# Shifting 128 rows by one partition: one transfer of 127 rows, or one of 126 and one of 1

## The reference

```
def shift_token(t):
    t1, t2 = jnp.split(t, 2, axis=-1)
    t2 = jnp.pad(t2, ((0, 0), (1, 0), (0, 0)))[:, :-1]
    return jnp.concatenate([t1, t2], axis=-1)
...
x = x + o @ wo
h = shift_token(x)
mu = h.mean(-1, keepdims=True)
var = h.var(-1, keepdims=True)
h = (h - mu) / jnp.sqrt(var + 1e-05) * lg + lb
h = h @ w1 + b1
a, g = jnp.split(h, 2, axis=-1)
h = a * jax.nn.gelu(g, approximate=False)
x = x + h @ w2 + b2
```

## Time and profile before

| | |
|---|---|
| time, median of 3 runs | 2962.85 us (2961.32 to 2963.24) |
| time of the profiled execution | 2961.68 us |
| its span, first to last instruction | 2959.4 us |
| busy, share of the span | PE 96%, DVE 74%, ACT 56%, POOL 35% |
| chain that ended last | PE 75%, DVE 11%, DMA 6% (`e_hs<-x` 4%), POOL 3%, ACT 2% |
| transfers into `e_hs` | 64 of 127 rows (63.5 KB), 56 of one row (0.5 KB) |

### The profile page before, as it was taken

One profiled execution on the slowest core, in us unless ns is written; L12 is line 12 of the kernel. 1 busy time (PEld: TensorE's weight loads), 2 busy tenths in 40 slices (PEclk: granted clock), 3 DMA queues, 4 the chain that ended last, 5 costly groups with the idle time before them and its releaser, 6 DMA issues.

```text
span 2959.4 us, 52471 instructions
## 1 busy us (share of the span) xinstructions
PE 2835.6 (96%) x20384; PEld 1908.3 (64%) x20384; DVE 2176.4 (74%) x5057; ACT 1653.3 (56%) x3488; POOL 1048.7 (35%) x1208
## 2 busy tenths in 40 slices
PE   8998999999999999999997899999999899999997
PEld 7777877333333333333336788888878788888886
DVE  7885545788788778868846777777867577788784
ACT  3222332665565666556664576666666666666662
POOL 5333432033113212511314344434454444444441
PEclk9999999999999999999997999999999999999998
DMA  2000010321321322132203000000010100000001
GB/s 78 23 9 22 8 22 3 43 24 17 35 26 12 39 24 26 17 46 26 37 1 98 5 5 5 4 5 5 11 37 14 31 21 4 18 5 12 12 11 59
DMA packets 46284, 66.64 MB, mean 23 GB/s; under 512 B 9662, under 2 KB 34260, under 8 KB 46036
## 3 DMA queue, kind: packets, MB, share of 16 engines
q1 hardware_dynamic: 46036, 63.29, 12.0%
HBM read 24.99 MB, written 8.39 MB: 11 GB/s over the span
## 4 chain that ended last, share of the span: by engine, by line
PE 75%; DVE 11%; DMA 6%; POOL 3%; ACT 2%; issue 1%; SPq 1%; POOLq 0%; DVEq 0%; ACTq 0%
PE ps L1394 17%; PE pw L218 13%; PE ps L218 11%; PE pw L1381 10%; PE ps L1180 5%; DMA e_hs<-x 4%; PE pw L1180 4%; PE ps L1554 4%; PE pw L1467 2%; PE pw L1505 2%; PE pw L1330 1%; PE pw L1487 1%; DVE stat L1837 1%; DVE e_ot L2132 1%; PE ps L1467 1%
## 5 line engine op out<-in xcount | busy, mean ns | idle before, releaser
L1682 ACT ACTIVATE c_p<-pw 128x512 f32<-128x512 f32 x1024 | 562.3, 595 | 341.2 <-PE ps L1364 183.5
L1394 PE MATMUL ps<-c_p,c_vals 128*64 128x512 f32 x2048 | 547.4, 618 | 2.7 <-ACT c_p L1682 1.4
L1968 DVE TENSOR_REDUCE c_mx<-ps 128x1 f32<-128x512 f32 x694 | 462.7, 683 | 114.3 <-PE ps L1364 106.7
L1381 PE MATMUL pw<-c_qst,c_kst 50*128 50x512 f32 x1024 | 385.1, 449 | 9.4 <-DMA c_qst<-c_mr 9.0
L1381 PEld LDWEIGHTS pw<-c_qst,c_kst 50*128 50x128 f32 x1024 | 154.5, 185 | 368.2 <-ACT c_p L1682 272.1
L1364 PE MATMUL ps<-c_kst,c_qst 48*128 48x512 f32 x694 | 289.5, 452 | 4.6 <-DMA c_kst<-shared 3.5
L1736 ACT ACTIVATE e_sm<-e_sm,e_mx 128x256 f32<-128x256 f32 x512 | 253.9, 498 | 62.0 <-DVE e_mx L2113 61.9
L1968 DVE TENSOR_REDUCE c_mx<-pw 128x1 f32<-128x512 f32 x330 | 225.5, 683 | 47.3 <-PE pw L1364 43.8
L2233 POOL TENSOR_SCALAR stat<-stat 128x1 f32<-128x1 f32 (+1 forms) x138 | 32.1, 233 | 623.4 <-DVE stat L1840 352.0
L1394 PEld LDWEIGHTS ps<-c_p,c_vals 128*64 128x64 f32 x2048 | 104.2, 135 | 181.2 <-issue 162.1
L218 PE MATMUL pw<-shared,e_xb 128*128 128x512 f32 x792 | 216.9, 412 | 2.2 <-DVE e_xb L2062 1.5
(11 more groups left out here) (316 smaller groups left out, 6441.0 us busy)
## 6 DMA issues: line engine op xcount, KB each, us to landing
c_kst<-shared SPq DMA_DIRECT2D x192, 64.0 KB
c_qst<-shared SPq DMA_DIRECT2D x64, 128.0 KB
x<-in_L_attn_x SPq DMA_DIRECT2D x8, 512.0 KB, 3.8
c_qst<-shared SPq DMA_DIRECT2D x64, 64.0 KB
keep<-x SPq DMA_DIRECT2D x8, 512.0 KB, 4.5
e_raw<-keep SPq DMA_DIRECT2D x8, 512.0 KB, 3.5
out<-x SPq DMA_DIRECT2D x8, 512.0 KB, 5.9
e_hs<-x SPq DMA_DIRECT2D x64, 63.5 KB
```

Source lines behind the costliest of these rows:

```text
L1381: e.matmul(bank_of("c_s", n, sh, kt, h), c_kst[i][p0:p0 + 50, sh // 2, 128 * kt:128 * kt + 128], c_qst[i][p0:p0 + 50, sh // 2, 512 * h:512 ...
L1394: ins = e.matmul(pv[64 * h:64 * h + 64, :], c_v[:, kt, 33 * hd:33 * hd + 64], p[:, 512 * h:512 * h + 512], start=kt == 0, stop=kt == 7, sk ...
L1682: e.activation(c_p[slot["c_p", (n, sh, kt)]][:, 512 * h:512 * h + 512], bank_of("c_s", n, sh, kt, h), ACT.Exp, scale=0.5).then_inc(SC, 1)
L1968: e.tensor_reduce(c_mx[m % 2][:, qt, h:h + 1], bank_of("c_max", n, sh, qt, h), AX.X, ALU.max).then_inc(VE, 1)
```

## The change

The 127 rows go as two transfers, 126 and 1, and the row of the tile above is issued last instead of first. The count that the waits look for rises by 16. The planner's 2.6 us stays.

```
-                    P.land(f"hs{slot['d_hs', (l, win)]}", 2 if win % 8 else 1, "d_hs", l, win)
+                    P.land(f"hs{slot['d_hs', (l, win)]}", 3 if win % 8 else 2, "d_hs", l, win)
...
                 w.wait_ge(*dve("d_wo", l, win))
+                e.dma_start(hs[1:127, :], x[0:126, win, 128:256]).then_inc(landed, 16)
+                e.dma_start(hs[127:128, :], x[126:127, win, 128:256]).then_inc(landed, 16)
                 if win % 8:
                     e.dma_start(hs[0:1, :], x[127:128, win - 1, 128:256]).then_inc(landed, 16)
-                e.dma_start(hs[1:128, :], x[0:127, win, 128:256]).then_inc(landed, 16)
```

## The result

| | before | changed |
|---|---|---|
| median of the runs | 2963.05 us (2961.32 to 2963.34) | 2921.60 us (2920.62 to 2922.86) |
| ratio, 95% interval | | 0.9862 (0.9844 to 0.9879) |
| time of the profiled execution | 2961.68 us | 2921.17 us |
| its span | 2959.4 us | 2919.3 us |

41 us faster, where 32 were forecast. On another chip (chip 9 of the experiments) the changed kernel came to about the same time, 2922.82 us, but the one before ran at 2956.69; the ratio there is 0.9883 (0.9869 to 0.9896), 34 us.

The account below looks back on a forecast made before the run. PE bounds the kernel, so only PE's gaps behind DVE's waits for shifted rows, or loads queued behind them, count: 24.6 us of gaps plus 6.3 of clock make 30.9, giving 2931 us, range 2918 to 2947.

Parts of the forecast that it names:

- One shift: Stage d, from SP's first issue until the shifted rows are there: 3.2 us instead of 5.61, 2.4 us earlier.
- first load: PE's gap of 6.17 us at 1612.37, behind a weight load sharing an engine with the 127 rows: 2.85 us gained.
- 1674: PE's gap of 2.58 us at 1674.42, where `e_rp` stands behind the statistics: 2.4 us gained.
- 2194: PE's gap of 1.62 us at 2194.36, `e_qn` right behind the statistics: the whole gap, 1.6 us, gained.
- gaps handed on: Rival, chance 0.18: PE meets ACT, POOL or a load a little later instead; half the sum, 2946 us.
- 2302: PE's gap of 4.84 us at 2302.88, where DVE waited 6.66 us for the shift: 2.9 us gained.
- the five equal gaps: Second layer, PE's gap of 1.77 us at 2465.14 and four alike every 83 us: 1.55 each, 7.75 us.
- last shift: PE's gap of 4.32 us at 2909.10, where `e_hf` stands behind the last shift: 2.4 us gained.
- The clock: Matmuls run slower after some PE gaps; with those gaps gone or short, 6.3 us come back.
- more than the gaps: Rival, chance 0.08: gaps left out shorten too and the clock stays up at both ends; 10 us more, 2921.
- the slower case: Rival, chance 0.04: last row comes later than the 127 rows did, beyond 1.38 us per issue and pause; 2984 us.
- Hidden anyway: Rival, chance 0.04: every gap moves to another wait within its block of four windows; within 5.9 us of before.

Follow-up runs that it names:

- chip 9: Second chip for the changed kernel, unaltered, against the kernel before: 2922.82 us against 2956.69, ratio 0.9883.
- 64 and 63: Changed kernel with the 127 rows split as 64 and 63 instead of 126 and 1, row of the tile above last: 2921.75 us, ratio 0.9880 against before.
- chips 11 and 9: Kernel before, unaltered, run again on chip 11: 2957.87 us, ratio 1.0001; changed kernel, unaltered, run again on chip 9: 2922.82 us.
- the one at a lower clock: Against the kernel before, only the order changed, 127 rows issued before the row of the tile above: 2944.25 us, ratio 0.9962; its profiled execution took 2968.94 us.
- 113 and 14 rows: Against the kernel before, the 127 rows go as 113 and 14, row of the tile above last: 2942.29 us, ratio 0.9947.

## Why the prediction was right, and what was mis-sized

**One shift.** Forecast 3.2 us, measured 3.14. Two errors met: the big issue takes 0.81 us and not 0.60, the last row is there 1.70 us after its issue and not 2.0. The reading by divisors held for 126 and 113 rows in the traffic, and for 64 and 63 in the time. By the Trainium skill's rule ("DMA: Bandwidth & Descriptors", "Why a DMA increments its semaphore by 16 and not by 1"), 126 rows go over 14 engines and 113 over one; the share of up to eight tenths and the 2.9 us at 22 GB/s agree. The Trainium skill's advice on the same page ("Rules for kernel authors") against two transfers to disjoint partitions gives as its reason that both halves use all 16 engines. One transfer of 127 rows doesn't, so the advice doesn't carry over: not splitting costs 34 to 41 us here. The Trainium skill's fixed cost of about 2.0 us on that page, from which the prediction worked out a loss of some 5 us, stands there as a fit for transfers issued from GpSimd; end to end these costs don't come, since three overlapping transfers from SP took 3.14 us.

**The gaps.** Forecast 24.6 us, measured 24.8 of PE's idle time. That close a sum is partly luck, since the single terms miss in both directions:
- first load: 2.85 forecast, 6.17 - 4.25 = 1.9. SP's load now starts 1.62 us after the first issue instead of 0.76, 0.86 later and not 0.58, since the big issue grew; and it lands 4.09 us after its issue, not 3.44 as when alone:

```profile
1602.43 17.35 SPq L2406 DMA_DIRECT2D e_raw<-in_L_ffn_w  x7
...
1606.52 0.42 ACT L1593 ACTIVATE e_w<-e_raw 124x256 fp32r<-124x256 f32 x1 [3.51 <-DMA e_raw<-in_L_ffn_w]
```

- 1674: 2.4 forecast, 2.58. 2238 and 2356: 1.25 and 1.3, both gone.
- 2194: 1.6 forecast. The gap is gone, but 0.95 for `e_pt` is new just before, and the wait for `e_xb` behind it grew from 1.2 to 2.22. So nothing was won at this place. This is the "gaps handed on" of the rivals, at one place.
- 2302: 2.9 forecast, 1.9. DVE still waits 4.26 us for this shift, where 6.66 were.
- the five equal gaps: 1.55 each forecast, 1.55 each measured (1.77 to 0.2). In the stretch 2409 to 2900, with the small waits, 13.7 of idle time became 1.9: 11.8, where the terms had about 9.6. The small waits there are worth more than counted.
- last shift: 2.4 forecast. 4.32 became 1.89 as forecast, but the next gap for `e_hp` grew from 1.95 to 2.84: 1.5.

**The clock.** This is the term that was mis-sized: 6.3 us forecast. PE's busy time fell by 12.8 us (9.9 between the profiles of chips 11 and 9), and the granted clock says how much of it is clock. The two levels are 1.00 (2.4 GHz) and 0.50 (1.2 GHz). Cut into slices of 1 us, the busy time of each slice times (1 - its clock) is an estimate, from the traces, of what the lower level added to PE's work: 23.8 us before and 13.4 after, so 10.4 less. By stage it is 2.4, 0, 3.1, 3.4 and 1.4 us less. On chips 11 and 9 it is 20.2 and 13.5, 6.7 less.

Where it came from, on the first chip: what the prediction counted whole came back, 1.5 us at 1674 and 3.4 after two of the five gaps. The low clock after 2302.88 it counted half and it went whole, 3.0 us. After 1612 and at the end, where it counted nothing, 1.0 and 1.4 came back. After the gap of 1.88 us at 2287.96 the clock fell too (0.57 from 2288 to 2292), which the prediction hadn't seen; the gap is still there, but the clock no longer falls, 1.7 us. Against that, the grown gap for `e_xb` at 2189.84 is followed by a low clock that is new, 1.7 us. At the end the 12 matmuls after the gap took 2.57 us at a clock of 0.59 and take 1.68 at 1.00 (the third column from the right):

```profile
2909.10:2911.67 2.57, 2.57 (x12) 2.27 (x12) 1.74 (x4) 0.00 (x0) 2.37 (x2) 0.59 1.03 344
```

```profile
2869.51:2871.19 1.68, 1.68 (x12) 1.47 (x12) 1.43 (x4) 0.00 (x0) 1.48 (x1) 1.00 1.03 343
```

The other 2.4 us of busy time (3.2 on chips 11 and 9) are not clock by this estimate, and open.

**The rest.** 2.5 us came from the stages before, with the same code; forecast was nothing. All profiled executions but the one at a lower clock reach the first shift between 1598 and 1604 us, whatever the kernel, so it is spread, not gain. The case that the prediction called "more than the gaps" (2921, chance 0.08) is what happened on the first chip in size and partly in cause; on chip 9 the change is worth 34 us, 2 from the forecast 32. The gaps are what the forecast earned. How near the total comes to it is in part luck, since the clock gives 10.4 us in one pair of profiles and 6.7 in the other.

**The rivals.** The 126 rows did spread. Three issues in a row took 2.0 us together and no 1.25 us each, the point of 1.38 per issue wasn't reached: the slower case is out, though single issues of up to 1.86 us exist. "Hidden anyway" is out by the stage table. Of the signs that the prediction named, one for being right missed, the first load (4.09 us and not 3.5), and one for being wrong showed at one place (the gap for ACT's `e_pt`). The block of four windows in the second layer takes 80.1 us where 81 was forecast, nearly the 79.8 of the first layer, where PE is the bound.

## What to carry to other kernels

Look at the row count of a transfer before its size: 127 rows on one engine took 3.25 us, 126 on many took 0.45, and cutting one row off was worth more than 1% of a kernel in which PE was 96% busy. Price a latency by the gaps of the bound engine, not by the waits of the one that sees it (130 us of DVE's waits were 25 us of PE's gaps), then add what a low clock after each gap costs; here that was 10.4 us on 24.8 in one pair of profiles and 6.7 on 23.9 in another, and the granted clock of short stretches shows it gap by gap. When a wait has been cut to where the bound engine hardly stops for it (3.1 us here), cutting it further gave nothing measurable, and telling the planner the true latency made the kernel 20 us slower instead of faster.

## What the runs showed of the hardware that was not expected

- The time to issue a transfer from SP doesn't follow its rows: 0.50 us for 64 rows, 0.54 for one row in 16 pieces, 0.60 for 127, 0.66 for 113, 0.75 for 63, 0.81 for 126, 0.86 for 14. The two whose largest divisor up to 16 is 14 are the dearest, and 64, which has 16, is the cheapest; why is open.
- The first 0.4 us per shift gave 12 us, 0.5 us gave 14, 2.5 us gave 34: the gain bends. In the 113 and 14 rows' profile it is PE's idle time that bends, not its clock.
- After five equal gaps of 1.8 us PE's clock fell to the lower level twice in one execution of before and once in another, each time at other gaps; after the five gaps of 1.2 us of the 113 and 14 rows it never fell.
